# Splitting the very last store by rows: 64, 15 and 49 rows in three transfers

## The reference, cut to what matters

```python
def reference(x, L0_conv_weight):
    ...
    def _gn(v, G=32, eps=1e-5):
        ...
        m = jnp.mean(g, axis=(2, 3, 4), keepdims=True)
        s = jnp.var(g, axis=(2, 3, 4), keepdims=True)
        return ((g - m) / jnp.sqrt(s + eps)).reshape(v.shape)
    ...
    x = x + _L0_conv_ref(_gn(x), L0_conv_weight)
    return x
```

## Time and profile before

| | us |
|---|---|
| median of 3 runs | 1858.06 |
| the runs | 1858.2, 1858.06, 1855.08 |
| profiled execution | 1858.08 |
| its span, first to last instruction | 1856.3 |

### The profile page before, as it was taken

One profiled execution on the slowest core, in us unless ns is written; L12 is line 12 of the kernel. 1 busy time (PEld: TensorE's weight loads), 2 busy tenths in 40 slices (PEclk: granted clock), 3 DMA queues, 4 the chain that ended last, 5 costly groups with the idle time before them and its releaser, 6 DMA issues.

```text
span 1856.3 us, 10200 instructions
## 1 busy us (share of the span) xinstructions
PE 1057.3 (57%) x2222; PEld 314.2 (17%) x2239; DVE 1337.8 (72%) x707; ACT 1096.5 (59%) x797; POOL 451.3 (24%) x380
## 2 busy tenths in 40 slices
PE   0999999999999756433343334333433343334332
PEld 0333333333333211100000000000000000000000
DVE  4899999999999999755565556655655565556554
ACT  0999999999999777534344434443444344434442
POOL 0777777777777500000000000000000000000000
PEclk9999999999999955555555555555555555555555
DMA  9999999999999999999999999999999999999998
GB/s 407 429 428 428 429 429 427 428 429 429 429 429 427 428 416 430 431 429 431 431 430 432 431 430 431 432 430 432 431 430 433 430 431 431 430 431 432 430 431 352
DMA packets 54892, 792.90 MB, mean 427 GB/s; under 512 B 6241, under 2 KB 6241, under 8 KB 6241
## 3 DMA queue, kind: packets, MB, share of 16 engines
q1 hardware_dynamic: 36000, 524.30, 66.3%
q10 hardware_dynamic: 18880, 268.48, 33.8%
HBM read 524.32 MB, written 268.44 MB: 427 GB/s over the span
## 4 chain that ended last, share of the span: by engine, by line
DMA 66%; DVE 16%; issue 6%; ACT 4%; POOL 3%; another core or an unknown queue 2%; PE 2%; SPq 0%; DVEq 0%; ACTq 0%; POOLq 0%
DMA out_dram<-ring 36%; DMA ring<-in_x_dram 31%; DVE square_maxs L493 6%; DVE ring L597 6%; POOL levels L298 3%; ACT levels L428 2%; PE product L640 1%; DVE first_sq_maxs L503 1%; DVE levels L591 1%; ACT ring L322 1%; ACT product L315 0%; PE product L636 0%; ACT product L341 0%; SPq L223 0%
## 5 line engine op out<-in xcount | busy, mean ns | idle before, releaser
L674 PE MATMUL product<-levels,w_lhsT 128*128 128x512 bf16 x1007 | 478.4, 626 | 705.2 <-DVE levels L591 701.9
L428 ACT ACTIVATE levels<-ring,tile_affine 128x2048 int16<-128x2048 f32 x240 | 490.2, 2087 | 586.6 <-DMA ring<-in_x_dram 573.9
L597 DVE SCALAR_TENSOR_TENSOR ring<-product,out_scale,ring 128x2048 f32<-128x2048 f32 (+1 forms) x258 | 600.2, 2327 | 0.1
L493 DVE TENSOR_REDUCE square_maxs<-ring 128x4096 f32 (+1 forms) x119 | 524.5, 4418 | 27.7 <-ACT ring L322 23.4
L298 POOL TENSOR_TENSOR levels<-ring 128x512 f32<-128x512 f32 x360 | 448.9, 1275 | 183.1 <-DMA ring<-in_x_dram 180.4
L591 DVE TENSOR_SCALAR levels<-levels 128x2048 bf16<-128x2048 int16 (+1 forms) x258 | 176.1, 683 | 439.7 <-ACT levels L428 437.6
L322 ACT ACTIVATE ring<-ring,group_stats 128x4096 f32<-128x4096 f32 x119 | 441.5, 3710 | 12.5
L640 PE MATMUL product<-levels,neg_mean 128*128 128x512 f32 x720 | 364.8, 617 | 12.2
L674 PEld LDWEIGHTS product<-levels,w_lhsT 128*128 128x128 bf16 x1024 | 110.3, 130 | 1072.5 <-DVE levels L591 818.3
L636 PE MATMUL product<-ring,neg_mean 128*128 128x512 f32 x480 | 236.7, 616 | 3.3 <-DMA ring<-in_x_dram 3.2
L640 PEld LDWEIGHTS product<-levels,neg_mean 128*128 128x128 f32 x720 | 118.7, 189 | 239.3 <-POOL levels L298 205.6
(11 more groups left out here) (83 smaller groups left out, 51.9 us busy)
## 6 DMA issues: line engine op xcount, KB each, us to landing
ring<-in_x_dram SPq DMA_DIRECT2D x250, 2048.0 KB, 16.2
out_dram<-ring ACTq DMA_DIRECT2D x126, 2048.0 KB, 43.5
out_dram<-ring ACTq DMA_DIRECT2D x4, 1024.0 KB, 7.2
levels<-in_L_conv_weight_dram ACTq DMA_DIRECT2D x2, 16.0 KB, 8.9
```

Source lines behind the costliest of these rows:

```text
L428: nc.scalar.activation(levels[:, h, :], halves[:, 2 * s + h, :], ACT.Identity, bias=tile_affine[:, a, 1, :], scale=tile_affine[:, a, 0, :] ...
L493: nc.vector.tensor_reduce(square_maxs[:, bass.ds(k + 1, 1)], ring[:, slot1(REST + g), :], AX_X, ALU.max).then_inc(maxed, 1)
L597: nc.vector.scalar_tensor_tensor(part, product[:, h, at], out_scale[:, :], part, ALU.mult, ALU.add).then_inc(combined, 1)
L674: mm = pe.matmul(product[:, h, n * BANK:(n + 1) * BANK], w_lhsT[:, :], ints[:, h, n * BANK:(n + 1) * BANK], start=True, stop=True)
```

## The change

The store of the last chunk of the last image is issued as three transfers one behind the other on ACT's queue, over rows 0 to 63, 64 to 78 and 79 to 127, where before it was one transfer of 128 rows. The wait ahead of it is the same. Each of the three counts 16 on the slot's semaphore, so SP's last wait for this slot asks for 32 more. All other stores and loads are left as they are.

```diff
+    LAST_ROWS = [slice(0, 64), slice(64, 79), slice(79, P)]
...
-                sp.wait_ge(stored[s], 16 * uses2(last // TC, last % TC))
+                extra = 16 * (len(LAST_ROWS) - 1) if last == CHUNKS - 1 else 0
+                sp.wait_ge(stored[s], 16 * uses2(last // TC, last % TC) + extra)
...
-            store(TILES - 1, TC - 1)
+
+            s = slot2(2, TC - 1)
+            act.wait_ge(combined, EXTRA + TILES * 2 * TC)
+            for rows in LAST_ROWS:
+                act.dma_start(out_rows[TILES - 1, TC - 1][rows, :], ring[rows, s, :]).then_inc(stored[s], 16)
```

## The result

The changed kernel takes 1864.45 us (median of 7 runs, 1862.4 to 1865.6) against 1857.93 us of the kernel before beside it (7 runs, 1855.08 to 1858.29): a ratio of 1.0035, interval 1.0025 to 1.0045, so 6.5 us slower. The forecast was 1856.2 us, with a range up to 1861.0. The profiled execution has a span of 1863.3 us, 7.0 more than before.

A forecast was written before the change was run, and what follows sets the result against it. The kernel is bound by moving bytes, its end by one late DMA engine. Issues and endings cost nothing, the row split gains 1.8 us: 1858.08 - 1.8 = 1856.3, 1856.2 against the median; range 1853.6 to 1861.0.

The forecast's parts named there:

- What bounds the kernel: Whole kernel bound by moving bytes; its end set by one DMA engine some 7 to 9 us behind.
- Issues and endings: Last store: two more issues on ACT of 0.338 us each and 38 to 48 endings instead of 16 cost nothing.
- Who carries which rows: Last store: seven engines carry 12 rows, eight carry 5, one carries 4, where all carried 8; 0.61 us per row.
- laggard: One of the last two DMA engines at work in the last store; the last goes on alone to 1855.2 us.
- if the last laggard is outside the seven: Last store: the late engine carries fewer rows, gain 1.3 to 2.4 us, taken as 1.8; chance 45 in 100.
- the seven: The seven engines expected to share the last store's 49 rows, 7 each, and so carry 12 rows, ending 2.4 us later.
- the rival of slower parts: Last store: parts run slower than a full store, gain 2.4 us to nothing, time 1855.7 to 1858.1; chance 12 in 100.
- Two of the rivals: Last store: laggard among the seven, 2.4 us more, 1860.5, chance 33 in 100; and slower parts, 1855.7 to 1858.1, 12.

The follow-up runs named there:

- the last experiment: Changed kernel's last store recut: all rows by 2560 columns, then rows 0 to 123 and 124 to 127 by the other 1536: 1859.29 us against 1858.07, ratio 1.0008.
- three parts by columns: Changed kernel's last store cut into 2048, 480 and 1568 columns, all 128 rows in each: 1858.69 us against 1858.16, ratio 1.0003.
- both stairs: Changed kernel's last store cut into 96, 11, 6, 5, 4, 3, 2, 1 rows, or 96, 7, 7, 6, 5, 4, 3: 1862.96 and 1863.81 us, one run each.
- the two halves: Changed kernel's last store cut into two transfers, rows 0 to 63 and 64 to 127: 1860.77 us against 1858.16, ratio 1.0024.
- the one piece: Changed kernel's code with the last store as one transfer of 128 rows again: 1858.24 us against 1858.16, ratio 1.0002.
- every second row: Changed kernel's last store cut into two transfers of 64 rows, the even rows and then the odd: 1858.13 us against 1858.07, ratio 0.9999.
- the shares spread out: Changed kernel's parts of 64, 15 and 49 rows kept, each taken by rows two apart: 1861.01 us against 1858.07, ratio 1.0017.
- the first stairs: Changed kernel's last store cut into eight transfers of 96, 11, 6, 5, 4, 3, 2 and 1 rows: 1862.96 us in one run.

## Why the prediction was wrong

**What bounds the kernel.** Right, and it is what the runs turn on: the end is one late DMA engine, and only what it carries or waits for counts, unless others are loaded past it as in the last experiment.

**Issues and endings.** Right: nothing, by the run with three parts by columns. The issues were longer than the 0.338 us that I took, and the backlog covered that as well.

**Who carries which rows.** The split was right: 16, 15 and 7 endings, 12 rows on the laggard's tail, and 124 rows on four engines in the last experiment. The Trainium skill's rule for the split (DMA: Bandwidth & Descriptors, section Why a DMA increments its semaphore by 16 and not by 1) agrees with each of these counts.

**The first step that failed** is "if the last laggard is outside the seven". It is one of them, the fifth engine in both stairs. I gave nine chances against seven on no row at all, and the sign of this term hung on it: 2.4 us more in place of 1.8 us less. The same page of the Trainium skill (section Latency and other measured facts) says that engines 7 and 15 are usually the slower ones; the two stairs show the fifth, so it doesn't hold here.

**The second is the rival of slower parts**, which I held to be another case, worth no loss, and which came on top. Its mechanism was right in the averages: while a part that lies in one half is under way, rows take 1.1 to 1.4 us on average, and they take 0.61 us when a part of as many rows is spread. The Trainium skill's section on the DMA port swizzle (SBUF — State Buffer, Door 1) says that bandwidth goes by the number of ports reached, and the averages, about half pace, agree with it. Single rows of 2.4 us stand in the change and in the two halves; why these are twice as slow again is open. Nor do the runs tell at which end of a transfer the rows crowd, as a row of the tile and its row in main memory go together in every cut. What I mis-sized is whom it hits. I let the laggard be alone by the time it reached the parts. But it is late with older rows while the others crowd, and these are held up: the unchanged store before the last landed 21.6 and 21.7 us after its issue in the change and in the two halves, 18.9 us before, in the one piece and by columns. Without crowding, or nearly so, the runs with every second row and with the shares spread out have 19.7 and 19.8 us, so up to 0.9 us of it may be scatter, and about 1.8 to 2.8 us are the price.

**The sum.** In the profiled executions the 7.0 us are made up so: the last store is issued 1.7 us later, the store before it lands 2.7 us later after its issue, and the laggard has 2.4 us of rows more, 6.8 together. So it comes to the last store at about 1862.3 - 12 x 0.61 = 1855.0, where the prediction has 1850.3. The 1.7 us don't come from the change, by the run with one piece. For the medians, 6.5 us apart, the runs that have one cause alone give 2.9 us (shares spread out) and 2.6 us (two halves), 5.5 together; about 1 us stays open, with the scatter and with the 15 crowded rows, whose share was not measured by itself. By the ratios, 3.2 and 4.5 us, the two make more than the whole, and the 4.5 hang on one long run.

**The range.** Two of the rivals together, 1860.5 and some 2.6 us, give 1863.1, beyond its upper end. I had treated as exclusive what could happen at once.

## What to carry to other kernels

When a kernel ends on its last transfers, count how many DMA engines are still at work in each stretch of one packet's length: if one engine is late, only its rows matter as long as no other is loaded past it, and a cut that gives some engines more must be known not to hit that one. If a tile must be cut by rows, a part should be spread over it (every second row) rather than be a block of neighbours; in these runs the block slowed its own rows and those of older transfers that were still under way. When two rivals rest on different mechanisms, give a range in which both happen.

## What the runs showed of the hardware

The late engine is the fifth, counted as in the stairs, in both executions that can number it, and it is 7 to 9 us behind 13 others in the profile before; why, no run here shows. It can stall while it is alone: in the first stairs the row that it starts after 1856.43 us takes 0.15 x 16 x 0.61 = 1.5 us with no other engine at work:

```profile
1856.43:1857.04 0.61, 0.00 (x0) 0.00 (x0) 0.00 (x0) 0.00 (x0) 0.00 (x0) 0.50 0.15 27
```

An issue of one part among several behind each other took 0.35 to 1.86 us on ACT with two or three parts, and 0.27 to 3.84 us with the eight of the first stairs, where the stores of the loop take 0.338 us; which of size, count of engines or the queue ahead makes it long was not taken apart.
